# The 48-row tail of the Silu experts' activation: both parts on one operand of the down product

## What is computed

```python
g = jnp.einsum('ecd,edf->ecf', xe, w_gate)      # d = 256, f = 176, c = 384
u = jnp.einsum('ecd,edf->ecf', xe, w_up)
ye = jnp.einsum('ecf,efd->ecd', jax.nn.silu(g) * u, w_down)
```

## Time and profile before

| | us |
|---|---|
| median of 3 runs | 1150.41 |
| lowest, highest | 1147.88, 1153.81 |
| span of the profiled execution | 1142.5 |
| its PE busy | 1058.0 (93%) |
| its DVE, ACT, POOL busy | 758.7, 599.1, 561.4 |
| down product of the experts (18 passes of 256 columns, x32) | inside 919 to 1119 |

### The profile page before, as it was taken

The page is one execution under the profiler, slowest core; times in us unless marked ns, Lnnn a source line. Parts: engine busy times, 40 slices in busy tenths (PEclk is TensorE's granted clock), DMA queues, the critical chain, the costliest instruction groups (busy, mean ns, idle before and its releaser), DMA issues. The chain is left out here.

```text
span 1142.5 us, 18205 instructions
## 1 busy us (share of the span) xinstructions
PE 1058.0 (93%) x6276; PEld 891.7 (78%) x6276; DVE 758.7 (66%) x1312; ACT 599.1 (52%) x1027; POOL 561.4 (49%) x408
## 2 busy tenths in 40 slices
PE   5899999999999999999998899997977988999992
PEld 4788888888888888888886776654765787999992
DVE  4877764787556775667775644466788655777777
ACT  3566653666536665446662423433532255777772
POOL 1664622756236563355540347762314776544453
PEclk9999999999999999999999999998998989999996
DMA  7700240002400762000000146641200457666666
GB/s 196 52 28 1 58 36 3 19 11 38 56 2 24 207 218 69 1 1 1 1 2 24 58 137 212 215 136 56 106 2 6 161 191 240 207 221 219 225 212 199
DMA packets 45642, 109.94 MB, mean 96 GB/s; under 512 B 8519, under 2 KB 26069, under 8 KB 43504
## 3 DMA queue, kind: packets, MB, share of 16 engines
q1 hardware_dynamic: 38640, 95.46, 30.2%
q0 software_dynamic: 6912, 13.30, 3.1%
HBM read 94.27 MB, written 41.29 MB: 119 GB/s over the span
## 5 line engine op out<-in xcount | busy, mean ns | idle before, releaser
L422 POOL TENSOR_TENSOR at_prob<-at_prob,at_inv_sum 128x1024 f32<-128x1024 f32 x128 | 243.6, 1905 | 287.9 <-DVE at_inv_sum L647 287.9
L612 ACT ACTIVATE at_pt_h<-ps 128x512 fp32r<-128x512 f32 x256 | 139.1, 596 | 148.7 <-PE ps L537 148.6
L697 DVE TENSOR_TENSOR at_pt_l<-ps,at_pt_h 128x512 fp32r<-128x512 f32 x256 | 164.6, 685 | 60.8 <-ACT at_pt_h L612 60.7
L686 DVE TENSOR_REDUCE at_neg_max<-ps 128x1 f32<-128x1024 f32 x128 | 156.1, 1220 | 42.1 <-PE ps L41 41.7
L579 ACT ACTIVATE at_prob<-ps,at_neg_max 128x1024 f32<-128x1024 f32 x128 | 143.7, 1123 | 18.1 <-DVE at_neg_max L686 18.1
L537 PE MATMUL ps<-ident,at_prob 128*128 128x128 f32 x1024 | 133.8, 274 | 3.8 <-POOL at_prob L422 3.8
L2072 POOL DMA_INDIRECT lines<-f_y,f_x_raw x96 | 95.8, 998 | 82.7 <-ACT f_y L1990 54.7
L537 PEld LDWEIGHTS ps<-ident,at_prob 128*128 128x128 f32 x1024 | 120.0, 141 | 20.9 <-POOL at_prob L422 4.7
L39 PE MATMUL ps<-at_k_h,at_q_h 128*128 128x512 f32 x256 | 108.8, 425 | 0.0
L41 PE MATMUL ps<-at_k_h,at_q_l 128*128 128x512 f32 x256 | 100.7, 393 | 0.0
L39 PE MATMUL ps<-at_pt_h,at_v_h 128*128 128x512 f32 x256 | 100.5, 393 | 0.0
(11 more groups left out here) (308 smaller groups left out, 2541.7 us busy)
## 6 DMA issues: line engine op xcount, KB each, us to landing
e_raw<-in_we SPq DMA_DIRECT2D x32, 624.0 KB, 4.2
f_cw_row<-cw SPq DMA_DIRECT2D x32, 512.0 KB, 4.7
slots<-in_empty SPq DMA_DIRECT2D x4, 3456.0 KB, 46.3
f_x_raw<-slots SPq DMA_DIRECT2D x32, 432.0 KB, 4.8
lines<-in_empty SPq DMA_DIRECT2D x3, 2048.0 KB, 33.8
f_e_raw<-in_we SPq DMA_DIRECT2D x32, 128.0 KB, 2.8
at_wq_raw<-in_wq SPq DMA_DIRECT2D x4, 512.0 KB, 3.5
at_wo_raw<-in_wo SPq DMA_DIRECT2D x4, 512.0 KB, 3.3
```

The costliest lines, as they stand in the source:

```text
L422: nc.gpsimd.tensor_tensor(prob[:, t % RING, :], prob[:, t % RING, :], inv_sum[:, t:t + 1].broadcast_to([P, T]), ALU.mult).then_inc(normed, 1)
L612: nc.scalar.activation(pt_h[:, e[1] % PT, :], turned(e[1]), ACT.Copy).then_inc(pt_high, 1)
L686: nc.vector.tensor_reduce(neg_max[:, t:t + 1], slot(n, start), AX.XY, ALU.max, negate=True).then_inc(maxed, 1)
L697: nc.vector.tensor_tensor(pt_l[:, e[1] % PT, :], turned(e[1]), pt_h[:, e[1] % PT, :].bitcast(F32), ALU.subtract).then_inc(pt_split, 1)
```

## The change

The body tile and the tail tile get separate operands. `a_h` and `a_l` keep the body alone (128x384 an expert). A new tile `a_t` holds the tail's low part on partitions 0 to 47 and its high part on partitions 64 to 111, the rest zero. The tail of the down weights is stored twice by the host, on the same two ranges of partitions, in the same array of the same size. One pass of `a_t` by the weights' high part then gives low by high and high by high together, and one pass of `a_t` by the weights' low part gives the two others: the tail takes two passes a block where it took three, and the block five where it took six. ACT gets a copy of 48x384 for the tail's high part, behind the body's Silu, which waits for L2225; DVE gets a subtraction of 48x384 for its low part, behind L2229, which waits for that copy. The wait for `down(n - 2)` moves from the body's copy to the tail's.

```diff
-        a_h, a_l = sb("a_h", [P, 2, 2, CAPACITY], F32R), sb("a_l", [P, 2, 2, CAPACITY], F32R)
+        a_h, a_l = sb("a_h", [P, 2, CAPACITY], F32R), sb("a_l", [P, 2, CAPACITY], F32R)
+        a_t = sb("a_t", [P, 2, CAPACITY], F32R)
+        TAIL_LOW, TAIL_HIGH = slice(0, REST1), slice(UPREST, UPREST + REST1)
...
+        def of_tail(n):
+            return SH1 + 2 * n + 1
+
         def of_act(n):
-            return SH1 + n + 1
+            return SH1 + 2 * n + 2
...
+                    body, tail = slice(DOWN1, DOWN1 + D), slice(DOWN1 + D, DOWN1 + 2 * D)
                     for b in range(SLOTS):
-                        for k in range(2):
-                            part = slice(DOWN1 + k * D, DOWN1 + (k + 1) * D)
-                            cols = slice(b * P, (b + 1) * P)
-                            last = product(nc, y_block(b), a_h[:, s, k, cols], a_l[:, s, k, cols],
-                                           e_h[:, r, part], e_l[:, r, part], k == 0, k == 1)
+                        cols = slice(b * P, (b + 1) * P)
+                        product(nc, y_block(b), a_h[:, s, cols], a_l[:, s, cols], e_h[:, r, body], e_l[:, r, body], True, False)
+                        nc.tensor.matmul(y_block(b), a_t[:, s, cols], e_h[:, r, tail], start=False, stop=False)
+                        last = nc.tensor.matmul(y_block(b), a_t[:, s, cols], e_l[:, r, tail], start=False, stop=True)
...
                         nc.scalar.activation(silu[:, s, 0, :], ps[:, 2, 0:CAPACITY], ACT.Silu).then_inc(silued, 1)
+                        act_e.wait_ge(timed, rest(n))
+                        if n >= 2:
+                            act_e.wait_ge(down_done, n - 1)
+                        else:
+                            act_e.wait_ge(consts, 71)
+                        nc.scalar.activation(a_t[TAIL_HIGH, s, :], act[TAIL_HIGH, s, 1, :], ACT.Copy).then_inc(act_high, 1)
...
                         act_e.wait_ge(timed, whole(n))
-                        if n >= 2:
-                            act_e.wait_ge(down_done, n - 1)
-                        nc.scalar.activation(a_h[:, s, :, :], act[:, s, :, :], ACT.Copy).then_inc(act_high, 1)
+                        nc.scalar.activation(a_h[:, s, :], act[:, s, 0, :], ACT.Copy).then_inc(act_high, 1)
...
-                nc.vector.memset(act[:, :, 1, :], 0.0).then_inc(consts, 1)
+                nc.vector.memset(a_t[:, :, :].bitcast(F32), 0.0).then_inc(consts, 1)
...
-                        nc.vector.tensor_tensor(a_l[:, p, :, :], act[:, p, :, :], a_h[:, p, :, :].bitcast(F32),
+                        nc.vector.tensor_tensor(a_l[:, p, :], act[:, p, 0, :], a_h[:, p, :].bitcast(F32),
...
-                        nc.vector.tensor_tensor(act[0:REST1, s, 1, :], ps[UPREST:UPREST + REST1, 4, 0:CAPACITY],
+                        nc.vector.tensor_tensor(act[TAIL_HIGH, s, 1, :], ps[UPREST:UPREST + REST1, 4, 0:CAPACITY],
...
+                        dve.wait_ge(act_high, of_tail(n))
+                        nc.vector.tensor_tensor(a_t[TAIL_LOW, s, :], act[TAIL_HIGH, s, 1, :], a_t[TAIL_HIGH, s, :].bitcast(F32),
+                                                ALU.subtract).then_inc(act_split, 1)
...
         w[:, 0:REST1, DOWN1 + D:] = down[:, P:F1, :]
+        w[:, UPREST:UPREST + REST1, DOWN1 + D:] = down[:, P:F1, :]
```

## The result

| | before | after |
|---|---|---|
| median, us (11 runs each) | 1150.41 | 1145.96 |
| lowest to highest, us | 1145.89 to 1153.89 | 1139.09 to 1149.25 |
| span of the profiled execution, us | 1142.5 | 1144.9 |

The ratio after to before is 0.9948, 95% interval 0.9928 to 0.9969: 6.0 us faster, between 3.6 and 8.3; the medians differ by 4.5. The sign was forecast and 1145.96 lies in the range, but 9.3 us were forecast. The changed kernel's profiled execution took 1146.87 us, so 2.0 us lie around its span.

A forecast was written before the change was run, and what follows sets the result against it. The prediction took PE to bound the kernel from expert 8 on; 9.0 us from 25 down products plus 0.3 at the end gave 9.3, taking the median from 1150.41 to 1141.1 us, range 1136.5 to 1147.0.

The forecast's parts named there:

- Bound and part 1: PE bounds the expert loop from expert 8; three passes fewer save 0.36 us a down product, 9.0 us over 25.
- Part 2, the round: ACT and DVE's new closed round of copies and subtractions lasts 5.57 us, under PE's new period of 5.59.
- Part 2, the time in hand: Activation's low part ends 3.2 us ahead of its down product, so a slightly longer round would not hold PE.
- The sign named beforehand: In the changed profile's expert loop, ACT waits for DVE or for PE by little.
- Rival 1: The round becomes the loop's pace if over 5.72 us; at 5.9 it gives 1145.3 us; chance 0.08.
- Part 4, the end: After the loop, the seed's end comes 0.2 us and down(30)'s end 0.36 earlier, its emptying about 0.3 earlier.
- The start, costed at nothing: Ahead of expert 7's turn, savings of down(0) to down(4), 1.8 us, become idling; that turn stays at 964.78.
- The time around the span: The profiled execution's span is 7.9 us under the median; the same was assumed around the new span of 1133.2.
- Rival 3, the clock: Longer PE idling puts half clock behind expert 7's turn at 964.78, costing some 1.5 us: 1142.6; chance 0.12.
- Rival 4: In the down products PE is paced by something else, such as weight loads; nothing changes: 1150.4; chance 0.02.

The follow-up runs named there:

- e2: Kernel before without the tail's pass of low activation by high weights, ACT and DVE unchanged: 1141.93 us, ratio 0.9922.
- e4: Changed kernel with one more ACT copy of 48x768, to a tile nothing reads, ahead of the tail's copy: 1164.27 us, ratio 1.012.
- e5: Changed kernel without the tail's two passes, leaving three passes a block: 1142.6 us.
- e11: Changed kernel run a third time, unaltered, for the spread: 1145.98 us, ratio 0.9958.
- e7: Changed kernel run again, unaltered, for a second trace: 1146.67 us, ratio 0.9945.
- e1: Changed kernel with the tail's copy placed behind high weights on ACT from n = 5 on: 1143.2 us, ratio 0.9938.
- e10: Changed kernel with the tail's copy behind high weights, run once more: 1143.04 us, ratio 0.9929.
- e8: Changed kernel with the tail's copy behind high weights and the last seed behind the emptying of down(30): 1142.04 us, ratio 0.992.
- e9: Kernel before run once more, unaltered, for a second trace: 1151.52 us.
- e3: Changed kernel with each block's last tail pass made twice, so PE has its old number of passes: 1150.23 us, ratio 1.0002.
- e6: Changed kernel without the tail's two passes and with the tail's copy behind high weights: 1129.88 us.

## Why the prediction was right or wrong, point by point

**Bound and part 1: right.** A pass removed is 0.12 us of distance (14 distances in 1.66 us are 0.119 each; six passes take the turns from 5.59 to 4.87, 0.120 each), turns are 5.59 apart while PE is the bound, and e2 gives 9.0 us, with an interval of 6.0 to 11.8 that makes the exact agreement luck. The 109 ns that the Trainium skill (TensorE: Matmul & The Clock Gate, section Back-to-back issue gap) gives for 256 columns does not agree with these rows. The same section of the Trainium skill calls its formula the distance of an isolated pass, too short at few columns, where it has no room for the weight load of each pass, and too long at many; the prediction did not say so.

**Part 2, the round: the mechanism was right, one term of its sum was mis-sized.** By the rows of one round after (timelines of DVE and ACT):

```profile
1099.12 0.51 ACT L2039 ACTIVATE f_a_h<-f_act 128x384 fp32r<-128x384 f32 x1
...
1099.66 0.56 DVE L2222 TENSOR_TENSOR f_a_l<-f_act,f_a_h 128x384 fp32r<-128x384 f32 x1 [1.10 <-issue]
1100.14 1.45 DVE L2192 TENSOR_TENSOR f_e_l<-e_raw,f_e_h 128x1248 fp32r<-128x1248 f32 x1
1101.50 0.95 DVE L2197 TENSOR_TENSOR f_x_l<-ps,f_x_h 128x768 fp32r<-128x768 f32 x1
1102.49 0.56 DVE L2234 TENSOR_TENSOR f_act<-ps,f_silu 48x384 f32<-48x384 f32 x1
...
1103.08 0.52 ACT L2028 ACTIVATE f_a_t<-f_act 48x384 fp32r<-48x384 f32 x1 [0.91 <-issue]
1103.63 1.25 ACT L1975 ACTIVATE f_e_h<-e_raw 128x1248 fp32r<-128x1248 f32 x1
1104.78 0.51 ACT L2039 ACTIVATE f_a_h<-f_act 128x384 fp32r<-128x384 f32 x1
```

The seven distances are 0.54 + 0.48 + 1.36 + 0.99 + 0.59 + 0.55 + 1.15 = 5.66. Forecast: 0.57 + 0.47 + 1.39 + 0.99 + 0.59 + 0.43 + 1.13 = 5.57. Six terms lie within 0.03. The tail's copy to high weights is 0.55, not 0.43: I took the overlap of two ACT instructions from L2017 to L1970, both with 128 partitions, and the tail's copy with 48 has none. That 0.12 turns "PE stays the bound, by a hair" around. Why there is no overlap is open: in e4 the copy of 48x768, shown as 0.84, is followed 0.75 behind its start by the tail's copy, so 48 partitions alone don't prevent it.

**Part 2, the time in hand: the wrong wait.** I measured it to the down product (3.2 us). The turn that stands behind the down product waits for DVE's low slots, as e5's rows name. It had about as much in hand: before, L2188 ends at 1014.29 + 0.96 = 1015.25, and the turn stands 0.12 behind the last pass at 1018.25, so 3.1 us. After, DVE's low slots at the beginning and in the middle:

```profile
975.96 0.96 DVE L2197 TENSOR_TENSOR f_x_l<-ps,f_x_h 128x768 fp32r<-128x768 f32 x1 [0.69 <-ACT f_x_h L2002]
...
1033.58 0.95 DVE L2197 TENSOR_TENSOR f_x_l<-ps,f_x_h 128x768 fp32r<-128x768 f32 x1
```

They end at 976.92, 1.90 us ahead of the turn at 978.82; ten experts on they end at 1034.53, 0.20 ahead of 1034.73. Turn by turn they are 1.90, 1.80, 0.74, 0.66, 0.60, 0.51, 0.45, 0.38, 0.32, 0.26 and 0.20 ahead: 0.06 to 0.10 goes in nine of the rounds, and 1.06 at once where ACT and DVE stand for marks of PE at 984 to 987 us (see the end, below). The stall is most of these 1.7 us; the prediction did not reckon with single stalls. Without them 24 rounds would have used 1.7 of 3.1 us, and by this sum PE would not have noticed. The cost was small all the same: from 1034.73 to 1109.20 are 13 turns, 74.47 us against 13 x 5.59 = 72.67, so 1.8 us, of which 0.83 is the wait for tokens; of the other two traces e11 has none, and e7 one of 0.39 at 1030.33. The pace sets in late or early by chance: 5.66 holds for the last five distances in e7 and for nearly all of the last sixteen in e11. The sign named beforehand, ACT waiting by little, failed too: ACT and DVE each wait 0.9 to 1.1 us an expert.

**Rival 1 came true in part.** Its condition, a round over 5.72, was not met, yet PE followed the round from 1034.73 on. The loop gave 7.7 us where 24 x 0.36 = 8.6 was forecast, so about 1 us of what is missing lies here, the round and the single stalls together; the runs do not part the two. E1 and e10, whose turns stay at 5.59, have a loop of 135.4 all the same: each has one stall of over 1 us near expert 8. e8 without it has 134.6 (24 x 5.59 = 134.2).

**Part 4, the end: wrong.** Forecast 0.3 us earlier plus down(30)'s 0.36; the end is 1.3 longer. ACT at the end of the loop (timeline, after):

```profile
1118.23 1.12 ACT L2005 ACTIVATE ps<-x 128x512 f32<-128x512 f32 x2
1119.38 0.53 ACT L2039 ACTIVATE f_a_h<-f_act 128x384 fp32r<-128x384 f32 x1
1119.81 0.58 ACT L2005 ACTIVATE ps<-x 128x512 f32<-128x512 f32 x1
1121.94 0.94 ACT L1995 ACTIVATE f_y<-ps 128x256 f32<-128x256 f32 x3 [1.54 <-remote]
```

PE beside it, down(30)'s last pass and down(31)'s first:

```profile
1119.60 0.27 PE L1955 MATMUL ps<-f_e_l,f_a_t 128*128 128x256 f32 x1
1123.02 0.36 PE L39 MATMUL ps<-f_e_h,f_a_h 128*128 128x256 f32 x1 [3.14 <-ACT f_y L1995]
```

and the same stretch of e1:

```profile
1116.56 0.58 ACT L2005 ACTIVATE ps<-x 128x512 f32<-128x512 f32 x1
1117.26 0.94 ACT L1995 ACTIVATE f_y<-ps 128x256 f32<-128x256 f32 x3
```

ACT stands for 1.54 us, in e7 for 1.48 and in e11 for 1.53, at the same instruction; before, e1 and e10 don't have it. It covers the 1.3 us. Down(30)'s last pass is shown to end at 1119.87, but ACT does have a wait open: for `down_done`, the mark that this pass makes. "Remote" stands for a mark that the profile could put down to no instruction. The trace's record of that semaphore has the step at 1121.91, 2.03 us behind the shown end of the pass, and ACT starts 0.02 behind the step. Down(29)'s mark came 0.02 behind its pass, and down(30)'s in the first trace of before too. ACT's other wait there, for the landed output of expert 24, had been met at 1118.88. So the mark was late, not ACT; down(31) on PE then waits for ACT in turn. Why the mark is late is open. The runs show that it is so in all three traces of this program, and that another order of two copies is without it (in e1 this mark is 0.39 late, and ACT stands for 0.12).

**The start, costed at nothing: wrong in size.** ACT's first silu of expert 1, PE's gate and up of expert 1 (first pass, and last pass of its tail), POOL's dispatches (timelines, after):

```profile
937.91 0.48 ACT L2019 ACTIVATE f_silu<-ps 48x384 f32<-48x384 f32 x1 [3.18 <-remote]
...
934.14 0.63 PE L39 MATMUL ps<-f_x_h,f_e_h 128*112 128x384 f32 x1 [3.52 <-issue]
...
935.84 0.53 PE L41 MATMUL ps<-f_x_h,f_e_l 128*112 128x384 f32 x1
...
940.14 0.97 POOL L2068 DMA_INDIRECT slots<-f_row,f_slot_of  x1 [2.61 <-PE ps L41]
```

ACT stands 3.2 us (3.21 and 3.25 in e7 and e11). For the first half of it PE is still at the tail's passes, which end at 936.37; the other 1.5 us are a late mark again, the one that these passes make. PE's own 3.52 us without work lie ahead of both (1.94 in before and in e9): there ACT's high part of the turned tokens started 1.6 us behind the turn's last pass. POOL's dispatches, which wait for PE's marks, lie still for up to 2.6 us. I had read PE's hold on POOL as 0.6 us, and the claim that none of this moves with PE was wrong. But e9, which is before's own code, has as much of it (waits, 915 to 970):

```profile
POOL slots L2059 <- PE ps L41: 2.7, 3, 1.7
```

So it does not belong to the new order. Turn 7 comes 51.6 us behind turn 0 in e2 and 50.6 in e3, and 47.8 in e8: the start scatters by program as much as the change moved it, so the 1.3 us can't be put down to the new order.

**The time around the span: wrong.** I took 7.9 us around it. It is 2.0 after, and 1.8 in e9; with 1.9 around its span the first profiled execution took about 1144.4 (an estimate from these two), less than any of before's runs on record, the quickest of which took 1145.89. It is also the only one of the thirteen traces in which no mark of PE comes late between 915 and 1130 us (see the last section), so the rows that the prediction was read from had none of the stalls that the others have. That shifts no difference, since the same was added on both sides, but a span compared with a median of other runs misled.

**Rival 3, the clock:** did not come. PE idles 4.59 us ahead of the turn of expert 5, whose transposes then take 1.54 us, at half clock (0.51 granted from 960 to 967); behind them PE waits 0.47 us for the tokens of expert 6, so this is hidden, and from expert 7 on the clock is 1.00. **Rival 4:** gone with 1.66 us for 15 passes.

## What to carry to other kernels

A new wait between two engines that already wait for each other closes a round: add up its start-to-start distances, and compare them with the period of the engine that bounds the kernel as it will be after the gain. Put the waiting instruction behind long work that waits for nothing: here moving one copy took 0.79 us an expert off where the round was the bound (e5, e6). And a margin counts to the first instruction that would wait, and must also carry single stalls, here of 1 to 3 us; a round forecast 0.02 us under a period of 5.59 was no margin, since one of its seven terms was 0.12 off.

The order of e1 (1143.2 and 1143.04 us) and e8 (1142.04) beats the kernel before by 7 to 9 us, and on the same chip the changed kernel by 2.9 and 4.6.

## What the runs showed of the hardware that was not expected

- Two ACT instructions in a row overlap in some pairs and not in others. The copy of 128x384 takes 0.51 to 0.53 us and the next starts 0.43 behind its start (1119.38 to 1119.81). The tail's copy of 48x384 takes 0.52 and high weights start 0.55 behind (1103.08 to 1103.63). But e4's copy of 48x768 takes 0.84 and the next, also with 48 partitions, starts 0.75 behind (1109.60 to 1110.35). What decides it is open; it has to be read from a row with the same two instructions.
- PE's marks can come late. From 915 to 1130 us of the three traces of the changed kernel 98 of 450 recorded steps of semaphores that PE raises come more than 0.2 us behind the shown end of the last pass that raises them, the longest 2.6 us; most others come 0.014 us behind. No step of a semaphore that ACT or DVE raises is late there (898 steps). In e1 four of PE's marks, 1.0 to 3.6 us late, come within 0.23 us of each other (980.16 to 980.39). The first trace of before has none (161 steps), the second has 29 of 150. In the three traces, in e9's and in e1's every wait of more than 0.3 us whose releaser the profile calls "remote" ends at such a mark. Nothing here shows the cause.
